# Six local-attention layers on one core: values moved by pairs of units, x loaded by DMA and turned by products, floor as a maximum of pairs, and another stage order

## What is computed

```
x = x + L0_xattn(layernorm(x), ctx)                # 16 heads of 8
x = x + L0_ffn(layernorm(x))                       # 16 experts, top 6
x = x + L1_xattn(ctx, layernorm(x))                # 8 heads of 64
x = x + L1_ffn(layernorm(x))                       # the six layers below

for i in range(6):                                 # x: 16 sequences of 128 tokens, 128 wide
    qkv = shift_tokens(x) @ Wqkv[i]                # 3 x 1024 columns, 16 heads of 64
    q, k = l2norm(q) * q_scale, l2norm(k) * k_scale    # t / max(norm(t), 1e-12)
    q, k = rotary(q), rotary(k)                    # with a position scale and its inverse
    out = softmax(8 * q k^T, in windows of 32 that look one window back) @ v
    x = out @ Wo[i] + x
    x = ffn_layer(shift_tokens(x), ...) + x        # layernorm, 128 -> 2 x 341, gelu gate, 341 -> 128
```

## Time and profile before

| | us |
|---|---|
| median of 3 runs | 2520.04 (2518.22 to 2523.63) |
| the profiled execution, its own time | 2516.71 |
| its span in the profile | 2514.9 |
| PE busy | 2202.2 (88%) |
| DVE busy | 1888.4 (75%) |
| ACT busy | 1644.5 (65%) |
| POOL busy | 1407.7 (56%) |
| mean granted TensorE clock | 0.961 of full speed |
| the moves of values (`stash<-l_v`) | 384 DMAs of 130 KB |

### The profile page before, as it was taken

How to read it: one execution, slowest core, us unless ns; L and a number is a source line. 1 busy time by engine, 2 the same in 40 slices (tenths; PEclk the granted TensorE clock), 3 DMA queues, 4 the chain that set the end, 5 groups by cost and what they waited for, 6 DMA issues and landing times.

```text
span 2514.9 us, 104113 instructions
## 1 busy us (share of the span) xinstructions
PE 2202.2 (88%) x36357; PEld 1707.3 (68%) x36357; DVE 1888.4 (75%) x4713; ACT 1644.5 (65%) x5384; POOL 1407.7 (56%) x2638
## 2 busy tenths in 40 slices
PE   6999699988999879998689986999878999889997
PEld 4775377767777557775577764777746777567775
DVE  4777688867888558886588865788756888578884
ACT  3554455557888458885478864788736887478883
POOL 3443511107777257774477753677635777267772
PEclk9997899988999989999899998999988999999999
DMA  3000000021111021111211111111111111011110
GB/s 93 0 0 1 1 0 0 0 69 32 30 34 34 18 63 34 29 30 27 54 35 34 29 32 45 35 34 34 27 50 31 34 34 33 11 42 32 33 35 24
DMA packets 58878, 76.12 MB, mean 30 GB/s; under 512 B 18262, under 2 KB 30692, under 8 KB 57956
## 3 DMA queue, kind: packets, MB, share of 16 engines
q1 hardware_dynamic: 58724, 74.13, 11.4%
HBM read 21.94 MB, written 1.05 MB: 9 GB/s over the span
## 4 chain that ended last, share of the span: by engine, by line
PE 54%; DMA 10%; SPq 8%; issue 6%; ACT 5%; DVE 3%; POOL 1%; ACTq 0%; DVEq 0%; POOLq 0%
PE bank L777 10%; DMA stash<-l_v 10%; SPq L354 7%; PE bank L841 5%; PE bank L794 5%; PE bank L786 4%; PE bank L861 4%; PE bank L821 4%; PE bank L851 2%; PE bank L716 2%; PE bank L804 2%; PE bank L919 2%; PE bank L909 2%; PE bank L908 2%; PE bank L705 2%
## 5 line engine op out<-in xcount | busy, mean ns | idle before, releaser
L497 POOL TENSOR_TENSOR l_qk<-l_rot 128x512 f32<-128x512 f32 x384 | 490.4, 1277 | 41.3 <-DVE l_rot L1562 41.1
L518 POOL TENSOR_TENSOR l_qk<-l_qk,l_rn 128x512 f32<-128x512 f32 x384 | 400.5, 1043 | 64.4 <-POOL l_rn L511 15.3
L777 PE MATMUL bank<-w_high,xs_part 128*128 128x512 f32 x768 | 355.8, 463 | 10.6 <-DVE xs_part L1549 9.6
L1138 ACT ACTIVATE prob<-bank,peak 128x64 f32<-128x64 f32 x1536 | 356.5, 325 | 1.8 <-DVE peak L1580 1.7
L1158 ACT ACTIVATE l_sq<-bank 128x512 f32<-128x512 f32 x384 | 236.0, 615 | 177.6 <-PE bank L777 169.3
L1558 DVE TENSOR_TENSOR l_rot<-bank,l_tab 128x512 f32<-128x512 f32 x384 | 264.1, 688 | 110.4 <-ACT l_sq L1158 109.6
L841 PE MATMUL bank<-l_v,probT 64*32 64x65 f32 x4608 | 180.2, 225 | 163.1 <-DMA stash<-l_v 156.5
L1174 ACT ACTIVATE l_qkT<-bank 128x512 f32<-128x512 f32 x384 | 230.2, 599 | 111.8 <-PE bank L794 106.1
L841 PEld LDWEIGHTS bank<-l_v,probT 64*32 64x32 f32 x4608 | 120.9, 108 | 238.1 <-issue 238.1
L794 PE MATMUL bank<-const,l_qk 128*128 128x128 f32 x1536 | 256.0, 290 | 13.4 <-issue 5.6
L1562 DVE TENSOR_TENSOR l_rot<-bank,l_tab 128x512 f32<-128x512 f32 x384 | 261.1, 680 | 0.0
(11 more groups left out here) (203 smaller groups left out, 5560.9 us busy)
## 6 DMA issues: line engine op xcount, KB each, us to landing
stash<-l_v SPq DMA_DIRECT2D x384, 130.0 KB
early<-in_L_ffn_Wqkv_dram SPq DMA_DIRECT2D x6, 1536.0 KB, 8.3
l_wo<-in_L_ffn_Wo_dram SPq DMA_DIRECT2D x6, 512.0 KB, 3.7
f_w<-in_L_ffn_W_dram SPq DMA_DIRECT2D x6, 341.0 KB
out_dram<-X SPq DMA_DIRECT2D x4, 256.0 KB, 2.3
f_w<-in_L_ffn_W_dram SPq DMA_DIRECT2D x6, 128.0 KB
l_oT<-in_L_xattn_Wkv_dram SPq DMA_DIRECT2D x1, 512.0 KB, 5.6
const<-in_const_dram SPq DMA_DIRECT2D x1, 392.0 KB, 3.4
```

The source lines that it names most:

```text
L497: pool.tensor_tensor(l_qk[:, k], l_rot[:, k, 0], l_rot[:, k, 1], ALU.add).then_inc(l["add_done"], 1)
L518: pool.tensor_tensor(v, v, l_rn[:, k, :, None].broadcast_to([128, 8, L_DIM]), ALU.mult).then_inc(l["qk_done"], 1)
L777: ins = pe.matmul(bank[:, 0, :].rearrange("p (q n) -> p q n", q=2), xs_part[:, part, j // 4], w[:, 0:2, 256 * g:256 * g + 256], start=n == ...
L1138: ins = act.activation(prob[:, k, n * BAND:(n + 1) * BAND], bank[:, 3 + r, p * BAND:(p + 1) * BAND], ACT.Exp, bias=peak[:, k, n:n + 1])
```

## The change

- **Values by pairs of units.** `move_values` runs twice per batch: after the second unit's v it moves the columns of units 0 and 1, after the fourth those of units 2 and 3. Each time it issues four DMAs of half the size. Each pair and each half of the buffers has a semaphore of its own, and `l_pv` waits at units 0 and 2.
- **Projection weights in pieces.** The next layer's 1.5 MB come in six DMAs of 512 columns, one behind each of the first six moves of a layer.
- **x by DMA.** SP copies a batch from Y to `xin` (`take_x`), two batches ahead, when `x_turned` says that the buffer is free; the first two of a layer after the first group of the feed-forward part.
- **x turned by products.** In place of a transposition there are two products, one for each half of the columns: with the identity, and with the shifting matrix, so that the token shift is made by PE. They go to bank 1, columns 256 to 383, beside the v projection's 0 to 255. ACT takes the high part from there in one copy and DVE the low part; xsT and two ACT copies are gone. In PE's list the stage goes from the sixth place to the last, and waits for the copy of the last v (`values_read`); the turning of q and k waits for its own bank alone.
- **Floor as a maximum of pairs.** The sums of squares go to every second element of a pair whose other element is 1e-24 from the start; a TENSOR_REDUCE takes the maximum of each pair into `l_s`.
- **Order.** POOL: refine, add, scale in place of scale, add, refine. ACT: log and the v copy come first, x after the copy of prob. DVE: the split of x first.
- Two waits before the first layer are placed differently, and the mask's semaphore is merged with another.

```diff
-            def move_values(ub, b, k):
-
-
-                sp.wait_ge(l["v_done"], upto(ub, 4 * b + 4))
+            def move_values(ly, b, k, q):
+
+
+
+                ub, two = ly * UNITS, slice(2 * q, 2 * q + 2)
+                sp.wait_ge(l["v_done"], upto(ub, 4 * b + 2 * q + 2))
                 apart(sp)
                 if not isinstance(b, int) or b >= 2:
-                    sp.wait_ge(l["pv_done"], upto(ub, 4 * b - 4))
+                    sp.wait_ge(l["pv_done"], upto(ub, 4 * b + 2 * q - 6))
                     apart(sp)
                 for dst, half, at in ((l_v2, 0, 32), (l_v2, 1, 32), (l_v3, 0, 64), (l_v3, 1, 0)):
-                    sp.dma_start(dst[64 * half:64 * half + 64, k], l_v[at:at + 64, k, half]).then_inc(moved, 16)
+                    sp.dma_start(dst[64 * half:64 * half + 64, k, two], l_v[at:at + 64, k, half, two])\
+                      .then_inc(moved[k][q], 16)
+
+            def take_x(ly, b, k):
+
+                sp.dma_start(xin[:, k], one(Y, b)).then_inc(ld_xin[k], 16)
+
+            def next_x(ly, b, k):
+                sp.wait_ge(l["x_turned"], upto(ly * B, b + 1))
+                apart(sp)
+                take_x(ly, b + 2, k)

             def serve_layer(ly, last):
-                ub = ly * UNITS
-                if not last:
-                    sp.wait_ge(l["w_split"], upto(0, (ly + 1) * W_CHUNKS))
-                    apart(sp)
-                    load_projections(ly + 1)
-                for b in range(2):
-                    move_values(ub, b, b)
-                with sp.Fori(1, B // 2) as i:
+
+                for b in range(4):
+                    for q in range(2):
+                        move_values(ly, b, b % 2, q)
+                        if q == 0:
+                            next_x(ly, b, b % 2)
+                        if not last and 2 * b + q < W_CHUNKS:
+                            if b + q == 0:
+                                sp.wait_ge(l["w_split"], upto(0, (ly + 1) * W_CHUNKS))
+                                apart(sp)
+                            load_projections(ly + 1, 2 * b + q)
+                with sp.Fori(2, B // 2 - 1) as i:
                     for k in range(2):
-                        move_values(ub, 2 * i + k, k)
+                        move_values(ly, 2 * i + k, k, 0)
+                        next_x(ly, 2 * i + k, k)
+                        move_values(ly, 2 * i + k, k, 1)
+                for b in range(B - 2, B):
+                    for q in range(2):
+                        move_values(ly, b, b % 2, q)
                 if not last:
                     sp.wait_ge(l["out_done"], upto(0, (ly + 1) * B))
                     apart(sp)
                     load_output(ly + 1)
+                    sp.wait_ge(f["y_done"], upto(0, ly * 4 + 1))
+                    apart(sp)
+                    for b in range(2):
+                        take_x(ly + 1, b, b)
                     sp.wait_ge(f["y_done"], upto(0, (ly + 1) * 4))
                     apart(sp)
                     load_feed_forward(ly + 1)
...
-            pool.memset(xsT[:, :, 0:1], 0.0).then_inc(preset, 1)
+            pool.memset(l_ss[:, :, :, 1:], 1e-24).then_inc(preset, 1)
...
-                return Pipeline(pool, [(4, l_scale), (3, l_add), (3, l_norm)], UNITS, UNROLL, 4)
+                return Pipeline(pool, [(4, l_norm), (3, l_add), (4, l_scale)], UNITS, UNROLL, 4)
...
-                def turns_read(mine, b, r):
-
-                    qk, x = (issued(mine, fn, r) for fn in (l_turn_qk, l_turn_x))
-                    pe.wait_ge(l["qkT_done"], upto(ub, no_more(4 * b + qk, UNITS)))
-                    pe.wait_ge(l["xs_done"], upto(2 * bb, 2 * no_more(b + (x + 3) // 4, B)))
+                def values_read(mine, b, r):
+
+                    v, x = (issued(mine, fn, r) for fn in (l_project_v, l_turn_x))
+                    pe.wait_ge(l["v_done"], upto(ub, no_more(4 * b + v, UNITS)))
+                    pe.wait_ge(l["x_split"], upto(bb, no_more(b + (x + 3) // 4, B)))
...
                 def l_turn_x(u, b, j):
+
                     if j % 4 == 0:
-                        pe.wait_ge(l["xin_done"], upto(bb, b + 1))
-                        turns_read(l_turn_x, b, 0)
-                        pe.transpose(bank[:, 2, 384:512], xin[:, j // 4], ident).then_inc(l["x_turned"], 1)
+                        x = xin[:, j // 4]
+                        pe.wait_ge(ld_xin[j // 4], (ly * B + b - j // 4) * 8 + 16)
+                        values_read(l_turn_x, b, 0)
+                        pe.matmul(bank[0:HALF, 1, 256:384], x[:, 0:HALF], ident, start=True, stop=True)
+                        pe.matmul(bank[HALF:, 1, 256:384], x[:, HALF:], shift_t, start=True, stop=True)\
+                          .then_inc(l["x_turned"], 1)
...
-                    pe.wait_ge(l["v_done"], upto(ub, u))
+                    values_read(l_project_v, b, j % 4)
...
-                    turns_read(l_turn_qk, b, j % 4)
+                    pe.wait_ge(l["qkT_done"], upto(ub, u))
...
-                    if j % 4 == 0:
-                        pe.wait_ge(moved, (ly * B + b + 1) * 64)
+                    if j % 2 == 0:
+                        pe.wait_ge(moved[j // 4][j % 4 // 2], (ly * B + b - j // 4) * 32 + 64)
...
-                stages = [(5, l_scores), (4, l_turn_qk), (6, l_pv), (1, l_project_qk), (1, l_project_v),
-                          (0, l_turn_x), (7, l_output), (6, l_turn_o), (5, l_turn)]
+                stages = [(5, l_scores), (4, l_turn_qk), (6, l_pv), (1, l_project_qk), (1, l_project_v), (7, l_output), (6, l_turn_o), (5, l_turn), (0, l_turn_x)]
...
                 def l_copy_x(u, b, j):
-
                     if j % 4 == 0:
-                        k = j // 4
                         act.wait_ge(l["x_turned"], upto(bb, b + 1))
-                        act.wait_ge(l["x_split"], upto(bb, b - 1))
-                        act.activation(xsT[0:HALF, k], bank[0:HALF, 2, 384:512], ACT.Copy).then_inc(l["xs_done"], 1)
-                        act.activation(xsT[HALF:, k, 1:], bank[HALF:, 2, 384:511], ACT.Copy).then_inc(l["xs_done"], 1)
-
-                        act.wait_ge(l["xs_done"], upto(bb * 2, b * 2 + 2))
                         act.wait_ge(l["v_proj"], upto(ub, u - 4))
-                        act.activation(xs_part[:, 0, k], xsT[:, k], ACT.Copy).then_inc(l["x_high_done"], 1)
+                        act.activation(xs_part[:, 0, j // 4], bank[:, 1, 256:384], ACT.Copy)\
+                           .then_inc(l["x_high_done"], 1)
...
-                return Pipeline(act, [(1, l_copy_x), (3, l_log), (7, l_copy_o), (6, l_copy_prob), (3, l_guess),
-                                      (2, l_copy_v), (4, l_copy_qk), (5, l_exp), (1, l_square)], UNITS, UNROLL, 4)
+                return Pipeline(act, [(3, l_log), (2, l_copy_v), (3, l_guess), (7, l_copy_o), (6, l_copy_prob), (1, l_copy_x), (4, l_copy_qk), (5, l_exp), (1, l_square)], UNITS, UNROLL, 4)
...
-                def l_copy_in(u, b, j):
-                    if j % 4 == 0:
-                        dve.wait_ge(l["x_turned"], upto(bb, b - 1))
-                        dve.tensor_scalar(xin[:, j // 4], one(Y, b), 1.0, None, ALU.mult).then_inc(l["xin_done"], 1)
-
                 def l_split_x(u, b, j):
                     if j % 4 == 0:
                         k = j // 4
                         dve.wait_ge(l["x_high_done"], upto(bb, b + 1))
-                        dve.tensor_tensor(xs_part[:, 1, k], xsT[:, k], xs_part[:, 0, k].bitcast(F32), ALU.subtract)\
+                        dve.tensor_tensor(xs_part[:, 1, k], bank[:, 1, 256:384], xs_part[:, 0, k].bitcast(F32), ALU.subtract)\
                            .then_inc(l["x_split"], 1)
...
                 def l_sum_squares(u, b, j):
                     k = j % 2
                     dve.wait_ge(l["sq_done"], upto(ub, u + 1))
-                    dve.wait_ge(l["rn_done"], upto(ub, u - 1))
-                    dve.tensor_reduce(l_ss[:, k], l_sq[:].rearrange("p (h n) -> p h n", n=L_DIM), AX.X, ALU.add)\
+                    dve.wait_ge(l["floored"], upto(ub, u - 1))
+                    dve.tensor_reduce(l_ss[:, k, :, 0], l_sq[:].rearrange("p (h n) -> p h n", n=L_DIM), AX.X, ALU.add)\
                        .then_inc(l["ss_done"], 1)
...
                 def l_floor(u, b, j):

                     dve.wait_ge(l["ss_done"], upto(ub, u + 1))
-                    apart(dve)
-                    dve.tensor_scalar(l_ss[:, j % 2], l_ss[:, j % 2], 1e-24, None, ALU.max).then_inc(l["floored"], 1)
+                    dve.wait_ge(l["rn_done"], upto(ub, u - 1))
+                    dve.tensor_reduce(l_s[:, j % 2], l_ss[:, j % 2], AX.X, ALU.max).then_inc(l["floored"], 1)
...
-                return Pipeline(dve, [(5, l_peaks), (1, l_split_x), (2, l_sum_squares), (0, l_copy_in),
-                                      (6, l_divide), (2, l_floor), (7, l_residual), (1, l_rotate)],
```

(1 more changed line is left out.)

43 lines of the change are left out of this document (24 added, 19 removed).

## The result

| | before | changed |
|---|---|---|
| median, us | 2519.13 (2514.32 to 2523.63, 4 runs) | 2387.34 (2385.23 to 2390.68, 4 runs) |
| the profiled execution, its own time | 2516.71 | 2385.23 |
| its span | 2514.9 | 2383.4 |
| mean granted TensorE clock | 0.961 | 0.968 |

The ratio is 0.9478, with a 95% interval of 0.9457 to 0.9499: 5.2% faster. The prediction said 2393.

The account below looks back on a forecast made before the run. PE's own work was taken to bound a slot, and four slots plus one wait for moved values a batch. 2516.7 - 112.0 - 6 - 22.0 + 10.6 + 3 = 2390.3, with 3.3 for the median 2393 us; range 2366 to 2440.

Parts of the forecast that it names:

- The waits inside a layer: PE's waits for the moves before the product with the values, 1.23 us in each of 91 batches, end: 112.0 us less.
- refill: PE drains and refills around each such wait; 0.07 per batch comes back, 6 us less (bounds 0 and 20).
- three slots of lead: Each pair's move starts three slots, 10.9 us for the first pair, ahead of its reader in PE, so waits end.
- Layer starts: With weights in pieces, four layer changes wait 4.5 us like the last one: 22.0 us less (bounds 10 to 30).
- + 10.6 for the products: On PE, two products of 0.11 replace one turning of x: + 0.11 per batch, 10.6 us (bounds 0 and 20).
- The draw at bank 1: Turning x last in PE's slot needs the last v copied out of bank 1: 0.03 per batch, 3 us (0 to 30).
- Rival 3: Float32 products of x cost four passes, each holding PE 0.21 in place of 0.11: 2413 us, chance 0.04.
- My nothing for it: DVE's floor falls from 0.61 to 0.18 us, none on PE's chain: worth nothing by itself, but room for the faster loop.
- Rival 1: Part of the gain turns into small waits, 0.15 us in each of some 360 steady slots, 54 us: 2447, chance 0.12.
- Rival 2: Moves stay on the path, as SP's queue runs late or pairs wait for an older product: 2452 us, chance 0.03.
- Rival 4: POOL's refining no longer fits beside PE's turning, so a unit takes 4.1 us: slower, 2530 us, chance 0.04.
- room of half a microsecond: In POOL's new order, refining takes 1.1 us and PE's turning 0.59, leaving half a microsecond; costed at nothing.

## Why the prediction was right, and where it was not

**The waits inside a layer (112 us).** Right in size. Five waits are left of 96, and the pairs alone, with only the 112 and a small refill in play, gave 124 (2520.1 - 2396.1; 119 between the two profiled executions). That is 7 to 12 for the refill where I took 6, inside my 0 to 20.

**The cause of it** was half told. I wrote that the three slots of lead end the waits. They do, but in this kernel the early copy of v together with the absence of x's copies does so as well, and I had not costed ACT's new order for the moves at all. So the change has two sufficient causes, and taking away the one that I believed in would have told me that it does nothing. Three runs show it together: late moves in the changed kernel (no loss), the pairs alone in the kernel before (124 us), and the early copy alone there (68 us), which is the other cause without the part that x has in it.

**Layer starts (22.0 us).** Right: 4.1 to 4.9 us each, and 23.6 us measured for one load in place of pieces. That the last layer's start would be the pattern for the others was the step that carried it.

**x: the term that was mis-sized.** I had + 10.6 for the products and 3 for the place, 13.6 us. With the pairs alone, where x is still turned in the old way, the two slots with x take 3.87 and 3.79 us; now they take 4.07. That is 0.20 to 0.28 per batch, 19 to 27 us, and one transposition in place of the two products gave 0.29 per batch back, 28 us. Two steps failed, and by luck one of them cost nothing.

The first is the reading of "PE bank L861 x4" in 0.45 us as four products of 0.11. The count in the chain is of instructions. A float32 product is two of them, as the 192 instructions on each of L802 and L803 show; so those 0.45 us were two products of 0.22. The Trainium skill (FP8 and Floating Point Precision, TensorE Precision Notes) gives four passes, by which I had worked out 0.21. The trace agrees with it after all, and what I wrote against it was wrong. But the halves of x run beside each other, which I had only as a lower bound. Four instructions in two steps of 0.11 would be 0.22 in place of 0.11, just the + 0.11 that I had.

The second is the spacing, which is in none of my terms. The records have 0.20, 0.16 and 0.20 us around and between the two steps where I had 0.11 for each. A slot with x is thus 0.47 longer than one without: 0.22 for two steps, and 0.25 for their spacing, 24 us in 96 batches. That is where the term went wrong. Rival 3 had 20 us for products of 0.21 that follow each other; they don't, so it came near the number by another mechanism.

**The draw at bank 1 (3 us)** is what the view names for the first of these gaps (the weight load's 81 waits in the steady loop), and the records speak against it. The copy of v ends 0.04 to 0.08 us behind the last turning's start, but the first product starts 0.20 behind it whether the copy ends sooner or later: 0.202 to 0.203 in 83 of the 84 batches where the one follows the other. Where the turnings of q and k (L831, 128x128) are followed by the small products with the values (L878) the step is 0.20 too, in 325 of 372 slots, and these don't wait for that copy. The single transposition, with the copy ending at the same point, starts 0.11 to 0.13 behind. So it looks as if PE takes the wider step where the shape of its tiles changes (the other changes of shape in the slot show 0.15), and the copy costs next to nothing. This is read from the records; no run has products of this shape in a place without the copy before them.

**What made up for it.** The pairs alone gave 124 us and the whole change 131.8, 8 more. The pieces are 23.6 of the difference and x takes 19 to 27 back; so 3 to 11 us are left for all the rest together, the new orders, the floor and the DMA of x, and no run takes them apart. PE's waits for the copy of v at the layer starts are a part, 13.3 us in the kernel before and 4.7 now. The floor's 10.7 us don't belong in this sum. They are what the old floor costs beside ACT's *new* list, and under the old list it costs nothing that the waits show, so the new floor only pays for the new order. My nothing for it holds against the kernel before; that the new order of ACT needs the shorter floor I had not seen. All in all x was 6 to 13 us too cheap, and the refill, the pieces and the rest gave 11 to 19 more than I had. The distance of 6 us between 2393 and 2387 is smaller than the errors in it, and that is luck.

**The steady loop** was to take 29.9 us for two batches and took 30.15. **Rival 1**, small waits in every slot, did not come: plain slots run at 3.60. **Rival 2**: SP's queue kept up. **Rival 4**: with POOL's old order nothing changes, and POOL's new 60.6 us of waiting for PE are slack, as its room of half a microsecond had said.

## What to carry to other kernels

Count the instructions per product in the code before taking a duration from a row with an "xN", because the chain counts instructions. When a wait goes, measure its lead, the time from the last producer to the reader, and not only whether the wait is there: here 1.1 us of lead decided, three edits moved it, and undoing the one that was meant to do it showed nothing. When a product is cut in two smaller ones, look at the starts of the records on both sides of them: here the spacing cost as much as the products. A wait of 5 us on PE cost more than its length here, with a lower clock behind it; moving a small DMA past a dozen large ones was worth 30 us. A small operation with a mean far above its minimum is waiting for something: look at the spread, and at what ends when it ends.
